# Two cross-attention layers on one core: the semantic term of three score tiles added by VectorE, a new order of the second layer's weight preparation, and q's first weights in two transfers

## The reference

```python
q = x @ Wq; k_text = text @ Wk; v_text = text @ Wv
text_out = attend(q, k_text, v_text)                       # softmax per head
scores = einsum('bhqd,bhkd->bhqk', q_h, ip_k_h) * scale    # ip_k = ip @ Wk_ip
text_probs = softmax(q @ k_text.T * scale)                 # one softmax over all channels
q_sem = text_probs @ text
sem = q_sem @ ip.T * scale                                 # (batch, 100, 645), the same for all heads
ip_probs = softmax(scores + 0.5 * sem[:, None]) * spatial_mask[:, None]
out = (text_out + ip_probs @ ip_v_h) @ Wout + bout + x
```

## Time and profile before

| what | value |
|---|---|
| median of 3 runs | 2004.28 us (2003.15 to 2005.21) |
| time of the profiled execution | 2001.58 us |
| its span, first to last instruction | 1999.8 us |
| PE busy | 1872.1 us, 94% |
| DVE busy | 1111.5 us, 56% |
| ACT busy | 778.4 us, 39% |
| POOL busy | 437.0 us, 22% |
| mean granted TensorE clock | 0.989 |

### The profile page before, as it was taken

How to read it: one execution, slowest core, us unless ns; L and a number is a source line. 1 busy time by engine, 2 the same in 40 slices (tenths; PEclk the granted TensorE clock), 3 DMA queues, 4 the chain that set the end, 5 groups by cost and what they waited for, 6 DMA issues and landing times.

```text
span 1999.8 us, 54230 instructions
## 1 busy us (share of the span) xinstructions
PE 1872.1 (94%) x23379; PEld 1488.3 (74%) x23379; DVE 1111.5 (56%) x2784; ACT 778.4 (39%) x1561; POOL 437.0 (22%) x522
## 2 busy tenths in 40 slices
PE   6988999999999999998889899999999999999998
PEld 3657788777778787884566688878787878888874
DVE  4775666667676767455631445455554545454542
ACT  3233454454454544442221333334343433343441
POOL 2032332433242424221000111111111112121210
PEclk9999999999999999999999899999999999999999
DMA  6651344343333342434263112323131413232211
GB/s 259 127 177 55 111 138 118 119 124 108 109 119 105 117 137 84 134 115 160 109 103 82 24 53 74 94 66 99 49 102 40 121 47 101 61 102 53 86 44 42
DMA packets 122167, 198.51 MB, mean 99 GB/s; under 512 B 40408, under 2 KB 109416, under 8 KB 115336
## 3 DMA queue, kind: packets, MB, share of 16 engines
q1 hardware_dynamic: 116600, 164.50, 29.3%
q10 hardware_dynamic: 5328, 30.54, 4.1%
HBM read 133.91 MB, written 60.88 MB: 97 GB/s over the span
## 4 chain that ended last, share of the span: by engine, by line
PE 71%; DMA 9%; DVE 8%; ACT 4%; POOL 3%; issue 3%; SPq 1%; ACTq 0%; POOLq 0%; DVEq 0%
PE proj L498 46%; PE proj L468 5%; PE pv L645 5%; DMA arena<-k_dram 4%; PE st L629 4%; PE rows L599 4%; DMA k_dram<-arena 3%; PE rows L498 3%; PE st L621 2%; PE rows L600 1%; DMA cbuf<-w_dram 1%; POOL cbuf L1186 1%; ACT arena L975 1%; POOL arena L1210 1%; DVE w_hl L1319 1%
## 5 line engine op out<-in xcount | busy, mean ns | idle before, releaser
L498 PE MATMUL proj<-w_hl,cbuf 128*128 128x128 f16 x9600 | 603.0, 219 | 0.7 <-issue 0.7
L498 PE MATMUL proj<-cbuf,w_hl 128*128 128x322 f16 (+1 forms) x3840 | 582.4, 301 | 6.4 <-DVE arena L1460 4.0
L498 PEld LDWEIGHTS proj<-w_hl,cbuf 128*128 128x128 f16 x9600 | 552.6, 98 | 11.6 <-issue 1.1
L498 PEld LDWEIGHTS proj<-cbuf,w_hl 128*128 128x128 f16 x3840 | 373.2, 97 | 179.6 <-DVE arena L1460 4.2
L1210 POOL TENSOR_TENSOR arena<-arena 128x400 f16<-128x400 f32 x240 | 235.4, 981 | 972.4 <-ACT arena L975 972.4
L974 ACT ACTIVATE arena<-st,rs 128x400 f16<-128x400 f32 x480 | 287.3, 599 | 410.7 <-PE st L629 276.6
L975 ACT ACTIVATE arena<-st,rs 128x400 f32<-128x400 f32 x480 | 285.8, 595 | 0.0
L951 ACT ACTIVATE arena<-proj 128x323 f16<-128x323 f32 (+1 forms) x160 | 70.7, 443 | 546.9 <-PE proj L498 531.0
L1508 DVE TENSOR_TENSOR arena<-arena 128x400 f16<-128x400 f32 x240 | 156.2, 651 | 224.5 <-ACT arena L975 218.9
L645 PEld LDWEIGHTS pv<-arena 128*128 128x128 f16 x4480 | 184.3, 96 | 60.7 <-POOL arena L1210 24.1
L645 PE MATMUL pv<-arena 128*128 128x66 f16 (+1 forms) x4480 | 198.7, 185 | 22.8 <-POOL arena L1210 19.0
(11 more groups left out here) (163 smaller groups left out, 1810.9 us busy)
## 6 DMA issues: line engine op xcount, KB each, us to landing
arena<-k_dram SPq DMA_DIRECT2D x240, 185.2 KB, 3.6
k_dram<-arena SPq DMA_DIRECT2D x80, 322.5 KB, 2.9
c_dram<-cbuf SPq DMA_DIRECT2D x16, 1290.0 KB, 7.2
raw<-ctx_dram SPq DMA_DIRECT2D x14, 1290.0 KB, 7.6
cbuf<-c_dram SPq DMA_DIRECT2D x12, 1290.0 KB
cbuf<-w_dram ACTq DMA_DIRECT2D x24, 640.0 KB, 6.2
arena<-q_dram SPq DMA_DIRECT2D x48, 125.0 KB, 2.6
cbuf<-c_dram ACTq DMA_DIRECT2D x2, 2580.0 KB
```

The costliest lines, as they stand in the source:

```text
L498: mm = nc.tensor.matmul(out, x[a](k), w[b](k), start=(k == 0 and m == 0), stop=(k == KT - 1 and m == 2))
```

## The change

In the second layer, score tiles 1, 3 and 5 lose their two semantic matmuls. A new DVE instruction, `add_semantic(u, j)`, reads the tile in PSUM, adds the transposed semantic term in f32 (`sem_t`, one copy for all four heads) and writes it back to the same place in PSUM. `exps` of these tiles waits for it (`s_sum`) and not for `s_full`. Once in a batch PE makes three f32 transposes of the semantic term (`turn_semantic`) into `rows` and ACT copies them to `sem_t`. `add_semantic` 1 is ahead of `prob_low` 0, 3 ahead of `prob_low` 2, 5 ahead of `prob_low` 4.

Between the layers, the splits of weights 2 and 3 are put in halves between the `kt_unit` and `vt_unit` on ACT and DVE, and `weight_turn` 2 and 3 later on PE. At the start `x_first` is the first transfer on SP, `wq` is loaded in two pieces (host side laid out by output tile), PE's first q tiles wait only for theirs, and not for `const`. In the last window `out_tile(1, 0, 4)` moves behind the last `weigh`, and on DVE behind `normalise`.

```diff
+ADDED = (1, 3, 5)
+        sem_t = sb("sem_t", [P, 2, len(ADDED), S], F32)
...
-            row_names += [("w", l, 3), ("q", l)] if l else [("ctx", 0), ("q", l), ("w", l, 3)]
-            row_names += [(n, 0) for n in ("logit", "pT", "ti", "semq")] if l else []
+            row_names += [("q", l), ("w", l, 3)] if l else [("ctx", 0), ("q", l), ("w", l, 3)]
+            row_names += [(n, 0) for n in ("logit", "pT", "ti", "semq", "semT")] if l else []
...
+                    row_names += [("semT", i + 1)] if ahead and g == 4 else []
...
+            sp.dma_start(x_first, x_d[0]).then_inc(x_in[0], 16)
             sp.dma_start(const[:], const_d).then_inc(const_in, 16)
...
 PE, score_tile and the new turn_semantic:
+                alone = l == 0 or j in ADDED
...
-                if l:
+                if not alone:
...
+            def turn_semantic(i):
+                pe.wait_ge(semq_ok, i + 1)
+                row_ready(pe, "semT", i)
+                for n, j in enumerate(ADDED):
+                    a = ip_cols(j)[0] - IPO
+                    mm = nc.tensor.transpose(rows[:, 0, n * S:(n + 1) * S], semq[i % 2][:, a:a + P], ident[0:S, 0:S])
+                mm.then_inc(row_full, 1)
 PE, window: between v_tile(n, 5) and score_tile(u, 4)
+                if ahead and g == 4:
+                    turn_semantic(i + 1)
...
                 if not more:
                     weigh(u, 3), weigh(u, 4), weigh(u, 5)
+                    if l:
+                        out_tile(l, 0, 4)
                     return
...
 PE, between the layers:
-            weight_turn(1, 2)
-            kt_unit(1, 0), kt_unit(1, 1), kt_unit(1, 2)
-            weight_turn(1, 3)
-            kt_unit(1, 3), kt_unit(1, 4)
-            turn(qs, q_chain, 6, "q", 1)
-            for t in range(TT):
-                vt_unit(1, t)
+            kt_unit(1, 0)
+            weight_turn(1, 2)
+            kt_unit(1, 1), kt_unit(1, 2), kt_unit(1, 3)
+            turn(qs, q_chain, 6, "q", 1)
+            kt_unit(1, 4), vt_unit(1, 0), vt_unit(1, 1)
+            weight_turn(1, 3)
+            vt_unit(1, 2), vt_unit(1, 3), vt_unit(1, 4)
...
             semantic(0)
+            turn_semantic(0)
             first_step(1)
 ACT, exps, and turn_semantic between v_unit(n, 0) and exps(u, 4) of g = 4:
+                if u >= STEPS and j in ADDED:
+                    act.wait_ge(s_sum, sums(u) + ADDED.index(j) + 1)
...
+            def turn_semantic(i):
+                row_filled(act, "semT", i)
...
+                nc.scalar.activation(sem_t[:, i % 2].rearrange("p n q -> p (n q)"), rows[:, 0, 0:len(ADDED) * S],
+                                     ACT.Copy).then_inc(row_free, 1)
...
-            act.dma_start(wq, wq_d[0]).then_inc(wq_in, 16)
+            act.dma_start(wq[:, 0], wq_d[0][:, 0]).then_inc(wq_first, 16)
+            act.dma_start(wq[:, 1:], wq_d[0][:, 1:]).then_inc(wq_in, 16)
...
 ACT, between the layers:
+            kt_unit(1, 0), kt_unit(1, 1)
+            split_weight(1, 2, (0, 1))
+            kt_unit(1, 2)
+            split_weight(1, 2, (2, 3))
             load_weight(1, 3)
+            kt_unit(1, 3), kt_unit(1, 4)
+            vt_unit(1, 0), vt_unit(1, 1)
+            split_weight(1, 3, (0, 1))
+            vt_unit(1, 2)
+            split_weight(1, 3, (2, 3))
+            vt_unit(1, 3)
             act.wait_ge(w_low, 32)
             fetch_context(1)
+            vt_unit(1, 4)
 DVE, the new instruction:
+            def add_semantic(u, j):
...
+                dve.wait_ge(s_full, u * NT + j + 1)
...
+                tile = st[:, j % 2, 0:Q4].rearrange("p (h q) -> p h q", h=HG)
+                term = sem_t[:, i % 2, ADDED.index(j)].unsqueeze(1).to_broadcast([P, HG, S])
+                nc.vector.tensor_tensor(tile, tile, term, ALU.add).then_inc(s_sum, 1)
 DVE, between the layers:
-            weight_parts(1, 2, range(4))
-            weight_max(1, 2)
             for c in range(CT):
                 q_part(1, 1, c)
             q_max(1)
+            weight_parts(1, 2, range(4))
+            weight_max(1, 2)
+            kt_unit(1, 0)
             weight_scale(1, 2)
-            weight_lows(1, 2, range(4))
-            kt_unit(1, 0)
-            weight_parts(1, 3, range(4))
+            kt_unit(1, 1)
+            weight_lows(1, 2, (0, 1))
+            kt_unit(1, 2)
+            weight_lows(1, 2, (2, 3))
+            kt_unit(1, 3)
+            q_scale(1)
+            weight_parts(1, 3, (0, 1))
+            kt_unit(1, 4)
+            weight_parts(1, 3, (2, 3))
+            vt_unit(1, 0)
             weight_max(1, 3)
...
+            vt_unit(1, 1)
+            weight_lows(1, 3, (0, 1))
+            vt_unit(1, 2)
+            weight_lows(1, 3, (2, 3))
+            vt_unit(1, 3)
             layer_scale(1)
+            vt_unit(1, 4)
```

More of the change, by code:

```diff
@@ L220, in on_pool, with sums @@
             return j in POOL_LOW
+        def sums(u):
+            return len(ADDED) * (u - STEPS)
         def low_done(eng, u, j):
@@ L467, in linear @@
                 for k in range(CT):
-                    mm = nc.tensor.matmul(bank[:, 0:MT], weight[:, k, c * P:(c + 1) * P], src[:, k],
+                    mm = nc.tensor.matmul(bank[:, 0:MT], weight[:, c, k], src[:, k],
                                           start=(k == 0), stop=(k == CT - 1))
@@ L472, in q_tile @@
             def q_tile(l, half, c):
+                if l == 0:
+                    pe.wait_ge(wq_in if c else wq_first, 16)
+                elif c == 0:
+                    pe.wait_ge(wq_in, 32)
                 if c == 0:
-                    pe.wait_ge(wq_in, 16 * (l + 1))
                     if l:
@@ L731, in window @@
                     v_tile(n, 5)
-                else:
+                elif l == 0:
                     out_tile(l, 0, 4)
@@ L768, in first_step @@
                 max_turn(u)
+            for c in range(4):
+                q_tile(0, 0, c)
             pe.wait_ge(const_in, 48)
             pe.wait_ge(ready, 2)
-            for c in range(4):
-                q_tile(0, 0, c)
             weight_turn(0, 0)
@@ L967, in exps @@
                 r = u // G
-                act.wait_ge(s_full, u * NT + (j + 1))
+                if u >= STEPS and j in ADDED:
+                    act.wait_ge(s_sum, sums(u) + ADDED.index(j) + 1)
+                else:
+                    act.wait_ge(s_full, u * NT + (j + 1))
                 low_done(act, u, j - 3)
@@ L1032, in window @@
                 split()
+                if l and i < B - 1 and g == 4:
+                    turn_semantic(i + 1)
                 exps(u, 4)
@@ L1110, in _ @@
             fetch_context(0)
-            split_weight(1, 2)
+            kt_unit(1, 0), kt_unit(1, 1)
+            split_weight(1, 2, (0, 1))
+            kt_unit(1, 2)
+            split_weight(1, 2, (2, 3))
             load_weight(1, 3)
-            kt_unit(1, 0), kt_unit(1, 1), kt_unit(1, 2)
-            split_weight(1, 3)
+            kt_unit(1, 3), kt_unit(1, 4)
[4 more added lines that the diff above has]
+            vt_unit(1, 3)
             act.wait_ge(w_low, 32)
             fetch_context(1)
-            kt_unit(1, 3), kt_unit(1, 4)
-            for t in range(TT):
-                vt_unit(1, t)
+            vt_unit(1, 4)
             for c in range(2):
@@ L1634, in window @@
                     logits(i + 1)
+                add_semantic(u, 2)
+                add_semantic(u, 3) if 2 not in ADDED else None
                 prob_low(u, 2)
+                add_semantic(u, 3) if 2 in ADDED else None
                 if ahead and g == 2:
@@ L1654, in window @@
                     out_tile(l, 0, 3)
-                    out_tile(l, 0, 4)
+                    if l == 0:
+                        out_tile(l, 0, 4)
                 if more:
@@ L1767, in _ @@
             q_max(1)
+            weight_parts(1, 2, range(4))
+            weight_max(1, 2)
+            kt_unit(1, 0)
             weight_scale(1, 2)
-            weight_lows(1, 2, range(4))
-            kt_unit(1, 0)
-            weight_parts(1, 3, range(4))
+            kt_unit(1, 1)
[8 more added lines that the diff above has]
+            vt_unit(1, 0)
             weight_max(1, 3)
-            kt_unit(1, 1), kt_unit(1, 2)
             weight_scale(1, 3)
-            weight_lows(1, 3, range(4))
-            kt_unit(1, 3), kt_unit(1, 4)
-            q_scale(1)
+            vt_unit(1, 1)
[3 more added lines that the diff above has]
+            vt_unit(1, 3)
             layer_scale(1)
-            for t in range(TT):
-                vt_unit(1, t)
+            vt_unit(1, 4)
             q_split(B)
@@ L1797, in _ @@
             normalise(2 * STEPS - 1)
+            out_tile(1, 0, 4)
             for c in range(CT):
```

28 lines of the change are left out of this document (20 added, 8 removed).

## The result

The changed kernel took 1992.2 us (median of 4 runs, 1988.5 to 1998.6) beside 2003.7 for the kernel before on the same chip: ratio 0.995 (0.9928 to 0.9971). The forecast was 1980, ratio 0.988; the time lies inside the range given, 1962 to 1995. (The ratios are those on record, with their 95% intervals; the quotient of the two medians can differ from them by 0.1%, here 0.994.) It was timed twice more later: 0.9912 (0.9899 to 0.9925) and 0.9956 (0.9939 to 0.9972). So the gain is 0.4 to 0.9%, 8 to 18 us, where 24 were forecast.

The account below looks back on a forecast made before the run. PE's own work was taken to bound the windows, with DVE just in time; between the layers PE waits. Gains 12.3 (windows) + 9.5 (between) - 0.4 (set-up) + 3 (end) = 24.4 us gave 1980; 8-in-10 range 1962 to 1995.

Parts of the forecast that it names:

- about 2 us because weight 3's transfers are issued 18 us later and share the DMA with the `kt` stores: Between the layers: a new loss of about 2 us, deducted from the 13.6 us to be saved there.
- the 9.5 us between the layers: Between the layers: 13.6 us of waits and slow clock removed, less 4.1 of new waits; bounds 12 and 3.
- a rival with a 4 us wait: Between the layers: stores, weight 3 and bank readings clash; gain 3 instead of 9.5 us, 1986 to 1987; chance 0.13.
- 13.6 - 0.7 - 1.4 = 11.5: Between the layers: 13.6 us saved; new waits of 0.7 at `weight_turn` 2 and 1.4 at `vt_unit` 2.
- done before the set-up's transfers: Between the layers: the second context's fetch moves by about 25 us and finishes before the set-up's transfers.
- The sum of 12.3 us for the windows: Second layer's windows: 8.9 in 24 ordinary, 4.8 in seven g = 3, 1.0 in the last, -2.4 in g = 4.
- D: Second layer's windows: price of one 128x400 f32 addition on DVE, taken as 0.63 us, between 0.57 and 0.89.
- hidden in the wait at `max_scores` 1: Ordinary windows: `k_part`'s wait for `v_unit(n, 0)` (done 1579.39, PE there at 1579.0) costs nothing extra.
- The rival of a dear addition: Second layer's windows: an addition takes 0.89 us, windows lose 2 us, whole gain about 10: 1994; chance 0.13.
- the slower one: Second layer's windows: an addition costs 1.08 us or more, cancelling the gain; at 1.3 us, 2017; chance 0.05.
- that all the saving arrives: Second layer's windows: DVE not late at `max_scores` 1, so the windows give 36 us: 1956; chance 0.12.
- Two signs that the prediction is wrong: Wait at `max_scores` 1 absent or over 1 us; a wait of 4 us staying between the layers.

Follow-up runs that it names:

- the small load: Changed kernel, loading only a sixteenth of the columns of the second layer's weight 3: 1974.5 us, ratio 0.9868; again 1979.9 us, 0.9892.
- the old order: Changed kernel with weights 2 and 3 each prepared whole and weight 3 loaded early, as before the change: 1987.1 us, ratio 0.9934; again 1990.5 us, 0.9947.
- the additions alone: Kernel before with only the DVE additions; sequence between the layers, start and end as before: 1990.0 us, ratio 0.9949.

## Why the prediction was right or wrong

**The step that failed** is "about 2 us because weight 3's transfers are issued 18 us later and share the DMA with the `kt` stores", in the 9.5 us between the layers. The clash was named, and as a rival with a 4 us wait, but priced too low. With the clash taken away by the small load, the stretch shortens by 10.5 and 10.2 us (130.9 to 120.4 and 120.7); the set-up costs some 0 to 0.5 in it (130.8 to 131.4 with the additions and the old order). So 13.6 - 0.7 - 1.4 = 11.5 was nearly sound. The clash itself costs 14.1 (134.5 - 120.4), 13.0 (133.7 - 120.7) and, on the kindest chip, 6.5 us (127.0 less 120.5, the mean of the two small loads, so across chips). Of the 14.1, 2.0 arose only behind the `vt_unit`s, and are not shown to be the clash's. The term as a whole, bounded at 3 from below, was -3.6, -2.8 and +3.9. What I left out was the chain: two `kt` buffers, so a late store holds ACT's `kt_unit` 4, and PE behind it. I had the median landing in mind (8.8 us over the ten stores), and the one that mattered was the one beside the load (20.3).

**`fetch_context(1)`**, "done before the set-up's transfers", was wrong too: issued at 1065.43 in the first profile, it was in flight during them. PE waited 2.29 us there for a key transfer, 1.50 before. That moving it gains time is shown only together with the halved splits, and across two chips: both moved, the stretch goes from 128.9 to 118.9.

**The pairs and the additions.** The sum of 12.3 us for the windows is near the 12.6 of the additions alone (841.0 to 828.4); 10.8 to 12.5 in the changed kernel's three profiles. But that is luck in good part, since its terms are right only together: 12.5 for the 24 ordinary windows where 8.9 was forecast, 1.1 for 4.8 in g = 3, 0.5 for 1.0 in the last, -1.3 for -2.4 in g = 4. Ordinary windows gave 0.52 instead of 0.37, chiefly since D was 0.58. g = 3 gave 0.15 instead of 0.68: `text_ip` needs the bank that `o_turn` frees, as I had written for g = 4 and not looked for there. g = 4 lost 0.19 instead of 0.34. And the place was wrong: of 0.50 us lost in an ordinary window 0.41 is at `k_part`, for `v_unit(n, 0)`, which I had as hidden in the wait at `max_scores` 1. The working had the pieces: a wait of 0.4 at `k_part` takes as much off the 0.65 at `max_scores` 1, yet I gave 0.6 there as a sign. The rival of a dear addition, and the slower one, fell with D = 0.58; that all the saving arrives fell with the windows.

**The signs.** Of what I said would show it, the rows of L629, the addition of 0.6, `exps` 3 at 8.1 (8.02) and the window (19.13 for 19.3) came; the wait of g = 4 was 1.78 and not 2. Two signs that the prediction is wrong came as well: the wait at `max_scores` 1 is all but absent, and a wait of over 4 us stays between the layers.

**Start and end.** The start gave 0.5 us where 0 was forecast, but it varies by more from profile to profile (166.3 to 169.1 us up to the first turn with the new start). The end gave 4.0 where 3: its last stretch starts 1.4 us earlier, not 3, and takes 2.5 less (17.06 for 19.58), a thing that I had only in the upper bound.

**Why 1992 and not 1980.** The term between the layers is short by 12.7 us in the first profile (-3.6 for +9.1) and 11.8 in the third, which is the gap of the medians. The first layer's 8 us in the profiled execution are no part of the change; its median of four runs lay 6 us below that execution. What makes the load hurt less on one chip stays open; over the same code a store packet took 0.037 us there, and 0.048 and 0.047 in the other two profiles.

## What to carry to other kernels

When a step is moved, follow its transfers to the buffers that must be free: here a large load beside small-packet stores took a store from 8.7 to 20.3 us, and a double buffer handed that to the engines. Put such a load behind the last store that anybody waits for, but look at who waits for the load then: moved by itself it gained nothing (1982.9 beside 1981.2 on one chip), and with its splits in halves, a later fetch and one addition fewer the kernel was 18 us below the changed one on another. Which of these did it was not taken apart. And moving work to a half-idle engine pays only as far as that engine's next hand-over: here taking one addition of three back to the full engine made ordinary windows 0.11 us shorter, and the median of the kernel with the load behind the stores 6 us lower (1982.9 to 1976.8).

## What the runs showed of the hardware

An in-place f32 addition of 128x400 in PSUM, one operand spread by a zero stride, takes 0.58 us, and DVE starts its next instruction 0.48 us after its start (1586.30 and, for `prob_low` 4, 1586.78 in the window above). A 192 KB store of 0.2 KB packets lands in 8.8 us by the median here, and in 13.6 and 20.3 us beside loads of 4.5 KB packets, which held ACT for 15.20 us. With the load cut to a sixteenth of its bytes in as many packets, the same store landed in 8.7 us at most. The same code of the first layer took between 739.4 and 755.4 us over the profiled executions of the study, mostly in waits of `max_scores` 0 for key transfers (18.2 us before, 24.3 in the first profile of the changed kernel), so one profile cannot tell 8 us there.
